# The patch stage of a ViT tower on one core: coarse levels gathered by matmuls with 0/1 matrices

## What is computed

```python
def _level(x, idx, W, b, p, gp):
    t = x.reshape(Bsz, C, h, p, h, p).transpose(0, 2, 4, 3, 5, 1).reshape(Bsz, h * h, p * p * C)
    t = t[:, idx]
    t = t.reshape(Bsz, h * h // gp, gp * p * p * C)
    return t @ W.T + b

Ws = [(idx0, W0, b0, 1), (idx1, W1, b1, 2), (idx2, W2, b2, 4)]
outs = [_level(x, idx, W, b, p, 16) for idx, W, b, p in Ws]
outs = [outs[0]] + [_interp_linear(o, n_tokens) for o in outs[1:]]
y = jnp.concatenate(outs, axis=-1)
return y @ Wf.T + bf
```

## Time and profile before

| | us |
|---|---|
| median of 3 runs | 814.07 |
| lowest and highest | 811.37, 817.34 |
| profiled execution | 815.75 |
| its span in the trace | 814.1 |
| TensorE busy (matmuls) | 713.6 |
| ScalarE busy | 223.5 |
| GpSimd busy | 141.5 |

### The profile page before, as it was taken

The page is one execution under the profiler, slowest core; times in us unless marked ns, Lnnn a source line. Parts: engine busy times, 40 slices in busy tenths (PEclk is TensorE's granted clock), DMA queues, the critical chain, the costliest instruction groups (busy, mean ns, idle before and its releaser), DMA issues. The chain is left out here.

```text
span 814.1 us, 11798 instructions
## 1 busy us (share of the span) xinstructions
PE 713.6 (88%) x4265; PEld 493.4 (61%) x4266; DVE 287.0 (35%) x618; ACT 223.5 (27%) x486; POOL 141.5 (17%) x194
## 2 busy tenths in 40 slices
PE   4587999999998889899999999989789989699960
PEld 3355854545455444389999998734535655477750
DVE  0003345454552598613233232036312152122211
ACT  2332124333332244244444441014200110122210
POOL 6761201011000053300000000000062113011023
PEclk9998999999999999999999999999679998799995
DMA  8318000000000030038888880035937821111002
GB/s 219 85 8 231 0 2 1 1 1 1 1 2 0 1 78 1 0 98 257 254 261 249 257 249 1 1 122 174 237 91 265 336 88 35 39 39 39 24 24 78
DMA packets 28087, 78.37 MB, mean 96 GB/s; under 512 B 7698, under 2 KB 17934, under 8 KB 26738
## 3 DMA queue, kind: packets, MB, share of 16 engines
q1 hardware_dynamic: 25090, 74.02, 30.7%
q0 software_dynamic: 2960, 3.84, 1.9%
HBM read 72.21 MB, written 5.63 MB: 96 GB/s over the span
## 5 line engine op out<-in xcount | busy, mean ns | idle before, releaser
L1358 PE MATMUL banks<-slots,soft_w 96*128 (+1 forms) x768 | 90.9, 275 | 1.6 <-PEq L1111 1.6
L1358 PEld LDWEIGHTS banks<-slots,soft_w 96*128 96x128 f32 x768 | 89.8, 192 | 1.8 <-issue 1.8
L1418 DVE COPY eo<-banks 32x192 f32 x128 | 45.3, 354 | 106.6 <-PE banks L1369 103.6
L1404 ACT ACTIVATE hid<-banks,soft_b 128x128 f32<-128x128 f32 x192 | 55.5, 368 | 61.4 <-PE banks L1358 61.3
L861 DVE TENSOR_REDUCE nm<-banks 128x2 f32<-128x906 f32 x48 | 53.0, 1103 | 44.2 <-PE banks L661 44.2
L1369 PE MATMUL banks<-soft_w,hid 128*128 128x192 f32 x384 | 67.5, 326 | 0.0
L825 ACT ACTIVATE pt<-banks 128x1024 f32<-128x1024 f32 (+1 forms) x48 | 49.0, 1023 | 58.5 <-PE banks L687 58.5
L1369 PEld LDWEIGHTS banks<-soft_w,hid 128*128 128x128 f32 x384 | 61.7, 190 | 0.0
L661 PE MATMUL banks<-kt,qt 32*128 32x453 f32 x192 | 49.4, 590 | 6.2 <-DVE nm L861 3.8
L82 PE MATMUL banks<-dense 128*128 128x512 bf16 x170 | 44.1, 414 | 11.0 <-PEq L2264 8.7
L687 PE MATMUL banks<-qa,kt 32*128 32x256 f32 (+1 forms) x384 | 51.5, 386 | 0.0
(11 more groups left out here) (267 smaller groups left out, 986.4 us busy)
## 6 DMA issues: line engine op xcount, KB each, us to landing
soft_w<-in_sw SPq DMA_DIRECT2D x64, 576.0 KB, 5.5
hy_band<-in_hband SPq DMA_DIRECT2D x6, 1540.0 KB, 6.6
switch_wi<-in_wi SPq DMA_DIRECT2D x1, 4608.0 KB, 24.9
switch_wo<-in_wo SPq DMA_DIRECT2D x1, 4608.0 KB, 16.3
hy_x_spread<-x_rows SPq DMA_DIRECT2D x24, 128.5 KB, 5.1
vt<-in_vt SPq DMA_DIRECT2D x1, 2496.0 KB
dwc_spread<-dispatch_cls SPq DMA_DIRECT2D x1, 1536.0 KB, 9.0
sorted_x<-zeros SPq DMA_DIRECT2D x16, 96.0 KB, 1.7
```

What stands on the lines that cost most here:

```text
L1358: mm = pe.matmul(ps[:, 2 * (r % 2) + j // 3, (j % 3) * P:(j % 3 + 1) * P], k.w1[r][:, d, j * P:(j + 1) * P], rhs, start=d == 0, stop=d == ...
L1404: ins = act.activation(hid[:, r % 2, j, :], ps[:, 2 * (r % 2) + j // 3, (j % 3) * P:(j % 3 + 1) * P], ACT.Gelu, bias=k.b1[:, ds(i * R + r, ...
L1418: dve.tensor_copy(eo[SL * r:SL * (r + 1), b, ds(i, 1), :].rearrange("p e d -> p (e d)"), ps[SL * b:SL * (b + 1), 4 + r, 0:D]).then_inc(eo_ ...
```

## The change

The two coarse levels are no longer gathered by indirect DMAs. Their rows are loaded in their own order (x1: 1024 rows in 8 tiles of 128, "sources"; x2: 256 rows in 2), and with them the index vectors as one row each, the same row on every partition, and a column that holds minus the number of each row. For every source ScalarE makes a 0/1 matrix: (index - number)^2, then relu(1 - that), which is 1 where the index names this row and 0 elsewhere. TensorE multiplies: level 1 by 8 matmuls per source with the matrix as the stationary operand, summed over the sources in bank 6 of PSUM (`pick1`); level 2 with the rows as the stationary operand, so that it comes out turned and its eight transposes go. Four matrices of level 1 exist at a time, so ScalarE waits for the picks of the source four before. GpSimd gathers only the pixels. The sums of phi's squares move behind the embedding of level 2, and their copy on ScalarE behind the last 0/1 matrix. TensorE gets 14 filling matmuls at its start, and FILL_TOK becomes 16.

```diff
--- before.py
+++ after.py
@@ -153,6 +153,9 @@
 
 E_TOK = 64
 G_TOK = 16
+SRC1 = 8
+SRC2 = 2
+HOT = 4
 FEAT = (3, 12, 48)
 ROWS = (4096, 1024, 256)
 
@@ -165,11 +168,14 @@
             return k.sb(name, shape, dt, st)
 
         idx0 = sb("idx0", [P, 32], I32)
-        idx1 = sb("idx1", [P, 8], I32)
-        idx2 = sb("idx2", [P, 2], I32)
+        row1 = sb("index_row1", [P, SRC1 * P], I32)
+        row2 = sb("index_row2", [P, SRC2 * P], I32)
+        source = sb("minus_source", [P, SRC1])
+        x1s = sb("x1_rows", [P, SRC1, B * 12])
+        x2s = sb("x2_rows", [P, SRC2, B * 48])
+        hot1 = sb("one_hot1", [P, HOT, SRC1 * P])
+        hot2 = sb("one_hot2", [P, SRC2, SRC2 * P])
         g0 = sb("g0", [P, 2, G_TOK, B * 3])
-        g1 = sb("g1", [P, 8, B * 12])
-        g2 = sb("g2", [P, 2, B * 48])
         g0b = sb("g0b", [P, 2, B, G_TOK * 3])
         g1b = sb("g1b", [P, B, 8 * 12])
         w0 = sb("w0", [48, E_TOK])
@@ -191,7 +197,10 @@
         w_in = k.sem("tok_weights_loaded")
         cls_zero, z_zero = k.sem("tok_cls_rows_zero"), k.sem("tok_z_zero")
         cls_in, bf_in = k.sem("tok_cls_loaded"), k.sem("tok_bias_row_loaded")
-        got2, got1, got0a, got0b = (k.sem(f"tok_gathered{n}") for n in ("2", "1", "0a", "0b"))
+        got0a, got0b = (k.sem(f"tok_gathered{n}") for n in ("0a", "0b"))
+        coarse_in, far1, far2, hot1_r, hot2_r, picked1_k = (
+            k.sem(f"tok_{n}") for n in ("coarse_loaded", "distance1", "distance2", "hot1", "hot2",
+                                        "picked1_source"))
         by1, by0 = k.sem("tok_by_image1"), k.sem("tok_by_image0")
         tr2, tr1, tr0 = (k.sem(f"tok_turned{i}") for i in (2, 1, 0))
         xt2, xt1 = (k.sem(f"tok_xt{i}") for i in (2, 1))
@@ -216,9 +225,12 @@
         with nc.Block() as block:
             @block.sync
             def _(sp):
-                sp.dma_start(idx2[:, :], a["idx2"]).then_inc(idx_in, 16)
-                sp.dma_start(idx1[:, :], a["idx1"]).then_inc(idx_in, 16)
                 sp.dma_start(idx0[:, :], a["idx0"]).then_inc(idx_in, 16)
+                sp.dma_start(source[:, :], a["minus_source"]).then_inc(coarse_in, 16)
+                sp.dma_start(row2[:, :], a["row2"].broadcast_to([P, SRC2 * P])).then_inc(coarse_in, 16)
+                sp.dma_start(row1[:, :], a["row1"].broadcast_to([P, SRC1 * P])).then_inc(coarse_in, 16)
+                sp.dma_start(x2s[:, :, :], a["x2"].rearrange("(k p) f -> p k f", p=P)).then_inc(coarse_in, 16)
+                sp.dma_start(x1s[:, :, :], a["x1"].rearrange("(k p) f -> p k f", p=P)).then_inc(coarse_in, 16)
                 sp.dma_start(k.ident[:, :], a["ident"]).then_inc(k.s_ident, 16)
                 phi.load(sp)
                 sp.dma_start(w2[:, :, :], a["tw2"]).then_inc(w_in, 16)
@@ -249,15 +261,7 @@
                 pool.memset(k.ones[:, :], 1.0).then_inc(k.s_ones, 1)
                 pool.memset(k.dense[:, :], 1.0).then_inc(k.s_dense, 1)
 
-                pool.wait_ge(idx_in, 48)
-                for j in range(2):
-                    pool.indirect_dma_start(g2[:, j, :], None, a["x2"],
-                                            bass.IndirectOffsetOnAxis(ap=idx2[:, j:j + 1], axis=0)
-                                            ).then_inc(got2, 16)
-                for j in range(8):
-                    pool.indirect_dma_start(g1[:, j, :], None, a["x1"],
-                                            bass.IndirectOffsetOnAxis(ap=idx1[:, j:j + 1], axis=0)
-                                            ).then_inc(got1, 16)
+                pool.wait_ge(idx_in, 16)
                 for j in range(G_TOK):
                     pool.indirect_dma_start(g0[:, 0, j, :], None, a["x0"],
                                             bass.IndirectOffsetOnAxis(ap=idx0[:, j:j + 1], axis=0)
@@ -287,15 +291,26 @@
                                        wf[:, 0, :], start=False, stop=q == 1)
                     mm.then_inc(hm, 1)
 
-                pe.wait_ge(k.s_ident, 16)
-                phi.column_sums(pe, 5)
-
-                pe.wait_ge(got2, 32)
-                for j in range(2):
-                    for b in range(B):
-                        mm = pe.transpose(ps[0:48, j, b * P:(b + 1) * P],
-                                          g2[:, j, b * 48:(b + 1) * 48], k.ident[:, :])
-                    mm.then_inc(tr2, 1)
+                def pick1(src):
+                    pe.wait_ge(hot1_r, src + 1)
+                    for j in range(SRC1):
+                        mm = pe.matmul(ps[:, 6, j * B * 12:(j + 1) * B * 12], hot1[:, src % HOT, j * P:(j + 1) * P],
+                                       x1s[:, src, :], start=src == j == 0, stop=src == j == SRC1 - 1)
+                    mm.then_inc(picked1_k, 1)
+
+                pe.wait_ge(k.s_dense, 1)
+                keep_busy(k, pe, 7, 14)
+                pe.wait_ge(coarse_in, 80)
+                pe.wait_ge(hot2_r, SRC2)
+                for b in range(B):
+                    for src in range(SRC2):
+                        mm = pe.matmul(ps[0:48, b // 2, b % 2 * 2 * P:(b % 2 + 1) * 2 * P],
+                                       x2s[:, src, b * 48:(b + 1) * 48], hot2[:, src, :],
+                                       start=src == 0, stop=src == SRC2 - 1)
+                    if b % 2 == 1:
+                        mm.then_inc(tr2, 1)
+                for src in range(4):
+                    pick1(src)
                 pe.wait_ge(w_in, 16 * 6)
                 pe.wait_ge(xt2, 2)
                 for g in range(G_TOK):
@@ -303,11 +318,17 @@
                                    w2[:, g, :], x2t[:, g // 8, :, (g % 8) * 16:(g % 8 + 1) * 16],
                                    start=g == 0, stop=g == G_TOK - 1)
                 mm.then_inc(ym2, 1)
+                phi.column_sums(pe, 5)
+                for src in range(4, 6):
+                    pick1(src)
                 pe.wait_ge(yr2, 1)
                 for b in range(B):
                     mm = pe.matmul(ps[96:112, 3 + b // 2, (b % 2) * D:(b % 2 + 1) * D],
                                    y2t[:, b * 16:(b + 1) * 16], wf[:, 2, :], start=True, stop=True)
                 mm.then_inc(zm2, 1)
+                for src in range(6, SRC1):
+                    pick1(src)
+                pe.wait_ge(k.s_ident, 16)
 
                 pe.wait_ge(by1, 1)
                 pe.wait_ge(phi.ss_r, 1)
@@ -370,18 +391,43 @@
                                    ps[:, h_bank(j, p), 0:2 * D].rearrange("q (b d) -> q b d", b=2),
                                    ACT.Copy).then_inc(hr, 1)
 
-                phi.squares(act)
-                phi.copy_sums(act, 5)
+                def one_hot1(src):
+                    if src >= HOT:
+                        act.wait_ge(picked1_k, src - HOT + 1)
+                    act.activation(hot1[:, src % HOT, :], row1[:, :], ACT.Square, bias=source[:, src:src + 1]
+                                   ).then_inc(far1, 1)
+                    act.wait_ge(far1, src + 1)
+                    act.activation(hot1[:, src % HOT, :], hot1[:, src % HOT, :], ACT.Relu, bias=1.0, scale=-1.0
+                                   ).then_inc(hot1_r, 1)
+
+                act.wait_ge(coarse_in, 80)
+                for src in range(SRC2):
+                    act.activation(hot2[:, src, :], row2[:, :], ACT.Square, bias=source[:, src:src + 1]
+                                   ).then_inc(far2, 1)
+                for src in range(SRC2):
+                    act.wait_ge(far2, src + 1)
+                    act.activation(hot2[:, src, :], hot2[:, src, :], ACT.Relu, bias=1.0, scale=-1.0
+                                   ).then_inc(hot2_r, 1)
+                for src in range(4):
+                    one_hot1(src)
                 for i in range(2):
                     act.wait_ge(tr2, i + 1)
-                    act.activation(x2t[:, i, :, :].rearrange("p b q -> p (b q)"), ps[0:48, i, :],
+                    act.activation(x2t[:, :, 2 * i:2 * i + 2, :].rearrange("p j b q -> p b j q"),
+                                   ps[0:48, i, :].rearrange("p (b j q) -> p b j q", b=2, j=2),
                                    ACT.Copy).then_inc(xt2, 1)
+                phi.squares(act)
+                for src in range(4, 6):
+                    one_hot1(src)
                 act.wait_ge(w_in, 16 * 6)
                 act.wait_ge(ym2, 1)
                 act.activation(y2t[:, :], ps[0:E_TOK, 2, 0:64], ACT.Identity, bias=tb[:, 2:3]).then_inc(yr2, 1)
-                act.wait_ge(got1, 128)
+                for src in range(6, SRC1):
+                    one_hot1(src)
+                phi.copy_sums(act, 5)
+                act.wait_ge(picked1_k, SRC1)
                 act.activation(g1b[:, :, :].rearrange("p b (j f) -> p b j f", j=8),
-                               g1[:, :, :].rearrange("p j (b f) -> p b j f", b=B), ACT.Copy).then_inc(by1, 1)
+                               ps[:, 6, 0:SRC1 * B * 12].rearrange("p (j b f) -> p b j f", j=8, b=B),
```

(8 more changed lines are left out.)

## The result

| | before | after |
|---|---|---|
| median of 4 runs each | 814.5 | 835.93 |
| lowest and highest | 811.37, 817.34 | 835.42, 836.85 |
| profiled execution | 815.75 | 835.42 |
| its span | 814.1 | 833.7 |
| TensorE busy (matmuls) | 713.6 | 738.5 |

The change makes the kernel slower: the ratio after / before is 1.0265, with a 95% interval of 1.0226 to 1.0305. The profiled executions differ by 19.7 us. Nearly all of it arises in the first stage; the windows and the timeline show where. (On two of the three chips of the experiments, part of the runs of the kernel before took 846 to 854 us instead of 829 to 839 us, and the ratios are formed without them.)

A forecast was written before the change was run, and what follows sets the result against it. The prediction took the ScalarE and TensorE chain ending the first stage as the bound. TensorE's 48.1 us queue from 11.4 us, less 4.0 us of filling, turned half 1 27 us later: 814.07 became 841 us, range 820 to 850.

The forecast's parts named there:

- What bounds: End of the first stage: a ScalarE and TensorE chain, then 4.0 us of unneeded filling, not the last gather.
- Rival 3: GpSimd's queue: the 12.5 us of issue taken off it count in full, 802 us; chance 0.02.
- Landing and start: Start of the first stage: coarse data land at 9.6 us, TensorE starts level 2 at 11.4 us.
- Rival 4: Coarse data land at 12 us or later, 3 to 6 us more, 845; counted within the forecast's 0.68.
- TensorE's queue: First stage: gathers of both levels plus moved work run back to back at the lower clock, 48.1 us.
- rival 2: Level 1's gather: clock rises for stretches or loads overlap better, half of 27.8 us goes, 828; chance 0.15.
- The clock does not stay up: TensorE in the first stage: it stays at 1.2 GHz under few-column matmuls, so level 1's gather costs 27.8 us.
- Rival 1: TensorE reaches 2.4 GHz early and stays there: 3.8 us faster than before, 810; chance 0.12.
- The weighing of the load's price: Level 1's gather: the trace's 0.217 us per load taken over the skill's 107 ns, which would give 827 us.
- ScalarE hidden, GpSimd's wait covered: First stage: ScalarE's 2.1 us per source hides behind TensorE's 3.5; GpSimd's wait of about 19 us costs nothing.
- From the gather to the end: After level 1's gather: 8.0 us to half 0 at 68.2, then the old chain; half 1 turned at 91.4 us.
- The end: Later stages: shifted and not changed, so half 1's turning 27 us later passes in full to the total.

The follow-up runs named there:

- before_fill16_third: The kernel before with FILL_TOK 16 in place of 34, on the third chip: 812.08 us, ratio 0.9951 to the kernel before.
- half_matrices: The changed kernel with ScalarE making only the first four level-1 matrices, TensorE still picking all eight sources: 850.88 us, ratio 1.0204 to the kernel before.
- before_fill16_again: The kernel before with FILL_TOK 16 in place of 34, another measurement: 845.75 us, four runs between 829.37 and 856.34, ratio 1.0153.
- bf16_picks: The changed kernel with bf16 0/1 matrices made by VectorE and rows as two bf16 parts: 823.71 us, ratio 0.9869 to the kernel before.

## Why the prediction was right, and where it was off

Forecast 841.0 us in a range of 820 to 850, with 0.83 for slower; measured 835.93.

- **What bounds.** Right. The last gather did not set the end of the stage: half 1 was regrouped from 84.21 us on, 23.7 us after its last gather had landed (60.52), and cutting the unneeded filling alone gained 4.0 us in the kernel before (before_fill16_third). Rival 3 (GpSimd's 12.5 us count in full, 802) falls with the measured time.
- **Landing and start.** Right: data at 9.88 us (9.6), TensorE at 11.54 (11.4). Rival 4 falls.
- **TensorE's queue.** The mechanism was right, the sum too high: 11.54 to 53.20 us is 41.7 us, forecast 48.1. The mis-sized terms are the two ahead of 26 us: level 2, 5.00 us instead of 6.9, and the first four sources, 9.64 instead of 13.9, together 6.2 us. The working took the lower clock for all of them; in fact it rose under level 2 at 14.3 us and stayed up to about 21.2. The forecast had this as rival 2 ("rises for stretches"), priced at half of the 27.8 us; of that sum 27.8 - 23.7 = 4.1 us went, so the truth lay between the forecast and rival 2, nearer to the forecast. The range covered both; that the time came within 5.1 us of the forecast rests on the mechanism, and the choice of the lower level for all of the queue was the part that failed. The others held: 3.67, 6.99, 2.74, and 14.1 for the last four sources (13.9).
- **The clock does not stay up.** Right: it fell while TensorE worked through 48-column picks without a gap, and the granted clock was 0.50 in every window from 25 to 65 us. Rival 1 needed the contrary. One reading behind this was wrong: TensorE was not busy for 4.09 of 5 us "and not less in the ten before" in the kernel before, but for 3.77 of the 5 us from 20 to 25. The conclusion that the stretch ran at the lower level rests on the durations and stands.
- **The weighing of the load's price.** Right to go by the row of 0.217 us: the last 64 instructions took 0.220. The Trainium skill (TensorE: Matmul & The Clock Gate, LDWEIGHTS) gives a load as its columns divided by 1.2, which makes 107 ns for 128 columns (an estimate from that page). By it the picks would have cost 13.7 us; they cost 23.7. The two would go together if each f32 instruction were two passes with a load each, 213 ns; the measured 0.220 fits that, but the trace records one load per instruction, so it is inferred and not shown. The same page of the Trainium skill (Part 1: The HAM clock gate) says that sustained activity releases the full clock. The trace agrees for 14.3 to 21.2 us, and not for 22 to 53 us, where TensorE was busy without a gap at 1.2 GHz.
- **ScalarE hidden, GpSimd's wait covered.** Right: 1.13 + 1.06 = 2.2 us per source against 3.5, half_matrices changes nothing in the picks; GpSimd idles from 22.8 to 37 us (forecast 24 to 43, the end earlier by what level 2 and the picks were), and its last gather landed by 60.52, long before 84.21.
- **From the gather to the end.** From level 1's regrouping to half 0: 53.72 to 61.70, 8.0 us, as forecast. Half 0 to the turning of half 1: 23.7 us, forecast 91.4 - 68.2 = 23.2; the keys took 4.29 us for 3.94, more of them at the lower clock.
- **The end.** 20.9 us at the turning of half 1 (27 forecast), less 1.2 us behind the stage, is the 19.7 of the profiled executions. The step that said "the later stages shifted and not changed" came out right to 1.2 us in the sum, which is partly luck: in between, the lag was down to 16.8 us.

## What to carry to other kernels

Moving a gather from the queue that issues it to TensorE pays only if that queue is what the end waits for; here the regrouped data lay 4 us before TensorE's queue was empty, so the first question is what stands ahead in the queue that consumes. A selection by 0/1 matrices is better done in two bf16 parts than in f32, where 16 bits of mantissa are enough: 5.2 instead of 23.7 us for the same 64 products. Against the kernel before neither gained. What did gain was to move work that the chain does not need yet (sums, spread, diagonals, norms, filling) behind it: 8 us by the medians, 4 of them accounted for by the traces.

## What was not expected of the hardware

- At 14.3 us the clock rose while TensorE worked on 256-column instructions with a stationary of 48 columns, and at 21.2 us it fell while 48-column ones ran without a gap. Before the change, TensorE worked from 11 to 35 us with little idle time and stayed at 1.2 GHz.
- On two of the chips, engines of the first stage stood idle with their inputs ready. Timeline of before_fill16_again:

```profile
11.16 6.96 PE L1013 MATMUL banks<-ones,phi_squares 96*128 96x1 f32 x32 [11.16 <-ACT phi_squares L1005]
...
40.85 0.18 ACT L1019 ACTIVATE phi_ss<-banks 128x8 f32<-128x8 f32 x1 [29.84 <-remote]
```

The sums that ScalarE copies were ready at 11.16 + 6.96 = 18.1 us, and it took them at 40.85. In the changed kernel on the same chip the pieces stood elsewhere, 4.1 us among the first picks and 9.16 us ahead of the turning of level 1. By the start of the next stage they add 14.4 us to the changed kernel (106.98 for 92.60 us), 8.7 to bf16_picks (80.95 for 72.21), and to the kernel before with less filling 18.1 us in one trace and 35.7 in the other (87.70 and 105.30 for 69.60). So their size differs between versions and between executions, which is why only durations of steps were compared there. What causes them stays open: they are absent on the third chip and in the first measurement, and no experiment addressed them.
